# Expert-bias mix of a routed layer as two float32r matmuls on split parts, remainders in the rows that held zeros

## The reference

```python
logits = jnp.einsum('th,eh->te', flat, router_weight) + router_bias
scores = jax.nn.softmax(logits, axis=-1)
topk_w, topk_idx = jax.lax.top_k(scores, K_TOP)
w_sum = topk_w.sum(axis=-1, keepdims=True)
w_dense = jnp.zeros((T, E), dtype=scores.dtype).at[jnp.arange(T)[:, None], topk_idx].add(topk_w)
bias_mix = jnp.einsum('te,eh->th', w_dense, expert_bias)
out = flat * w_sum + bias_mix
```

## Time and profile before

| | before |
|---|---|
| median of 3 runs | 1754.7 us (1750.4 to 1756.32) |
| profiled execution | 1754.61 us, of it span 1752.8 us |
| PE | 1696.2 us busy, 97% of the span |
| PE weight loads | 1427.7 us, 81% |
| DVE | 871.8 us, 50% |
| ACT | 778.8 us, 44% |
| POOL | 298.5 us, 17% |
| mean granted TensorE clock | 0.992 |

### The profile page before, as it was taken

How to read it: one execution, slowest core, us unless ns; L and a number is a source line. 1 busy time by engine, 2 the same in 40 slices (tenths; PEclk the granted TensorE clock), 3 DMA queues, 4 the chain that set the end, 5 groups by cost and what they waited for, 6 DMA issues and landing times. The chain is left out here.

```text
span 1752.8 us, 25373 instructions
## 1 busy us (share of the span) xinstructions
PE 1696.2 (97%) x8546; PEld 1427.7 (81%) x8546; DVE 871.8 (50%) x2683; ACT 778.8 (44%) x2143; POOL 298.5 (17%) x669
## 2 busy tenths in 40 slices
PE   5888999999999999999999999999999999999999
PEld 4667897888888888888888888888888788888887
DVE  7776010555555555555556546556566553323212
ACT  4476434555455455445445536545545432121111
POOL 4611000221131122122112113112222000000000
PEclk9989999999999999999999999999999999999999
DMA  5200425111111101101101101100100231000000
GB/s 158 72 1 1 156 80 208 37 25 37 37 25 36 37 24 38 37 13 49 37 13 49 37 13 41 38 20 17 45 13 19 80 95 43 1 24 1 24 1 24
DMA packets 47001, 74.73 MB, mean 43 GB/s; under 512 B 4576, under 2 KB 23008, under 8 KB 44832
## 3 DMA queue, kind: packets, MB, share of 16 engines
q1 hardware_dynamic: 45984, 72.63, 13.0%
q10 hardware_dynamic: 896, 0.56, 0.1%
HBM read 52.20 MB, written 20.97 MB: 42 GB/s over the span
## 5 line engine op out<-in xcount | busy, mean ns | idle before, releaser
L961 POOL TENSOR_SCALAR prob<-prob,inv_sum 128x128 f32<-128x128 f32 x256 | 98.5, 385 | 829.3 <-DVE inv_sum L1104 829.3
L1199 PE MATMUL ps_q<-h_hi,kv_w_hi 128*128 128x512 f32 x512 | 205.7, 402 | 1.4 <-PEq L758 1.4
L989 ACT ACTIVATE prob<-prob,neg_max 128x128 f32<-128x128 f32 x256 | 100.7, 393 | 238.4 <-DVE neg_max L1099 238.4
L1199 PE MATMUL ps_q<-h_lo,kv_w_hi 128*128 128x512 f32 x512 | 200.1, 391 | 0.0
L1199 PE MATMUL ps_q<-h_hi,kv_w_lo 128*128 128x512 f32 x512 | 199.8, 390 | 0.0
L133 ACT ACTIVATE prob_t_hi<-ps_s 128x512 fp32r<-128x512 f32 x192 | 107.4, 598 | 73.9 <-PE ps_s L1248 73.9
L962 POOL TENSOR_SCALAR prob<-prob,inv_sum 128x256 f32<-128x256 f32 x256 | 136.9, 535 | 0.0
L1084 DVE TENSOR_TENSOR x<-ps_q,x 128x512 f32<-128x512 f32 x128 | 88.3, 690 | 97.6 <-PE ps_q L1277 97.6
L138 DVE TENSOR_TENSOR prob_t_lo<-ps_s,prob_t_hi 128x512 fp32r<-128x512 f32 x192 | 126.2, 685 | 15.1 <-ACT prob_t_hi L133 12.5
L1466 DVE SCALAR_TENSOR_TENSOR f_act<-f_ps_r,f_scale,f_act 128x512 f32<-128x512 f32 x44 | 33.0, 751 | 192.1 <-PE f_ps_r L1497 190.7
L991 ACT ACTIVATE prob<-prob,neg_max 128x256 f32<-128x256 f32 x256 | 127.2, 497 | 0.0
(11 more groups left out here) (184 smaller groups left out, 4244.8 us busy)
## 6 DMA issues: line engine op xcount, KB each, us to landing
k_scratch<-kv_stage SPq DMA_DIRECT2D x32, 256.0 KB, 2.4
v_scratch<-kv_stage SPq DMA_DIRECT2D x32, 256.0 KB, 2.0
w_raw<-in_wq_g SPq DMA_DIRECT2D x8, 1024.0 KB, 4.8
k_raw<-k_scratch SPq DMA_DIRECT2D x32, 256.0 KB, 3.5
v_raw<-v_scratch SPq DMA_DIRECT2D x32, 256.0 KB, 4.0
w_raw<-in_wo_g SPq DMA_DIRECT2D x8, 1024.0 KB, 6.2
x<-in_x SPq DMA_DIRECT2D x16, 256.0 KB, 2.9
out<-x SPq DMA_DIRECT2D x16, 256.0 KB, 2.1
```

The source lines that it names most:

```text
L961: pool.tensor_scalar(prob[:, b, h, 0:P], prob[:, b, h, 0:P], inv_sum[:, b, h, 0:1], 1.0, ALU.mult, ALU.mult)
L989: act.activation(prob[:, b, h, 0:P], prob[:, b, h, 0:P], ACT.Exp, scale=-1.0, bias=neg_max[:, b, h, 0:1], accum_out=row_sum[:, b, h, 0:1])
L1199: last = pe.matmul(ps_q[:, h % 2, :], wq[a][:, c, h * HEAD:(h + 1) * HEAD], h3[b][:, c, pair * PAIR:(pair + 1) * PAIR], start=(c == 0 and ...
```

## The change

The mix becomes two float32r matmuls. The expert biases are loaded twice, into rows 0 to 63 and 64 to 127. Once, at the stage's start, ACT rounds all 128 rows to float32r, and DVE replaces rows 64 to 127 by the remainder. `chosen` is written twice side by side (128 columns), so that after the transpose rows 64 to 127 of `chosen_t` repeat rows 0 to 63. ACT's copy rounds it to float32r; DVE subtracts the rounded part from the transposed weights in PSUM and writes the remainder of 64 rows into `chosen_lo`. Then one matmul over 128 rows gives rounded weights times (rounded + remainder of the biases), and a second over 64 rows adds the remainder of the weights times the rounded biases. The fourth product, of both remainders, is left out. A new semaphore `b_ctl_done` is set by DVE's subtraction; PE waits for it before the mix and, in place of `b_ctc_done`, before it writes the shared bank again. The two memsets of zeros are gone.

```diff
--- before.py
+++ after.py
@@ -463,7 +463,8 @@
     def load(self, eng, router_t, router_bias, expert_bias):
         eng.dma_start(self.router[:, :, :], router_t.rearrange("(c p) n -> p c n", p=P)).then_inc(self.loaded, 16)
         eng.dma_start(self.logit_bias[:, :], router_bias.partition_broadcast(P)).then_inc(self.loaded, 16)
-        eng.dma_start(self.expert_bias[0:EXPERTS, :], expert_bias).then_inc(self.loaded, 16)
+        for rows in (slice(0, EXPERTS), slice(EXPERTS, P)):
+            eng.dma_start(self.expert_bias[rows, :], expert_bias).then_inc(self.loaded, 16)
 
 
 class RoutedBias:
@@ -492,7 +493,9 @@
         self.one_zero = sb("r_one_zero", [P, 2], F32, st)
         self.combined = sb("r_combined", [P, 2, 2], F32, st)
         self.chosen = sb("r_chosen", [P, 2, P], F32, st)
-        self.chosen_t = sb("r_chosen_t", [P, 2, P], F32, st)
+        self.chosen_t = sb("r_chosen_t", [P, 2, P], F32R, st)
+        self.chosen_lo = sb("r_chosen_lo", [P, P], F32R, st)
+        self.bias_parts = sb("e_bias_parts", [P, HID], F32R, st)
         self.ps_t, self.ps_l, self.ps_m, self.ps_n = [bank[:, n, :] for n in range(4)]
         self.ps_c = self.ps_t
         self.zeroed = sem("b_zeroed")
@@ -512,6 +515,8 @@
         self.scaled_done = sem("b_scaled_done")
         self.ct_done = sem("b_ct_done")
         self.ctc_done = sem("b_ctc_done")
+        self.ctl_done = sem("b_ctl_done")
+        self.bias_hi_done, self.bias_lo_done = sem("b_bias_hi_done"), sem("b_bias_lo_done")
         self.mix_done = sem("b_mix_done")
         self.x_done = sem("b_x_done")
         self.h_next_done = sem("b_h_next_done")
@@ -523,15 +528,22 @@
         return self.ps_n.rearrange("p (c n) -> p c n", c=KC)
 
     def set_constants(self, pool):
-        for n, (part, value) in enumerate(((self.one_zero[:, 0:1], 1.0), (self.one_zero[:, 1:2], 0.0),
-                                           (self.weights.expert_bias[EXPERTS:P, :], 0.0), (self.chosen[:, :, EXPERTS:P], 0.0))):
+        for n, (part, value) in enumerate(((self.one_zero[:, 0:1], 1.0), (self.one_zero[:, 1:2], 0.0))):
             if n:
                 pool.wait_ge(self.zeroed, n)
             pool.memset(part, value).then_inc(self.zeroed, 1)
 
     def await_constants(self, eng):
-        eng.wait_ge(self.zeroed, 4)
-        eng.wait_ge(self.weights.loaded, 48)
+        eng.wait_ge(self.zeroed, 2)
+        eng.wait_ge(self.weights.loaded, 64)
+
+    def bias_hi_part(self, act):
+        hi_part(act, [self.bias_parts[:, :]], self.weights.expert_bias[:, :]).then_inc(self.bias_hi_done, 1)
+
+    def bias_lo_part(self, dve):
+        dve.wait_ge(self.bias_hi_done, 1)
+        low = self.bias_parts[EXPERTS:P, :]
+        lo_part(dve, [low, low], self.weights.expert_bias[EXPERTS:P, :]).then_inc(self.bias_lo_done, 1)
 
     def pool_body(self, pool, i, par, live):
         if live(6):
@@ -599,7 +611,8 @@
             dve.wait_ge(self.rest_done, t3 + 1)
             if not known(t3) or t3 >= 2:
                 dve.wait_ge(self.ct_done, t3 - 1)
-            dve.tensor_tensor(self.chosen[:, odd, 0:EXPERTS], self.e[:, odd, :], self.rest[:, odd, :], ALU.subtract).then_inc(self.chosen_done, 1)
+            twice = [part[:, odd, :].unsqueeze(1).to_broadcast([P, 2, EXPERTS]) for part in (self.e, self.rest)]
+            dve.tensor_tensor(self.chosen[:, odd, :].rearrange("p (n e) -> p n e", n=2), twice[0], twice[1], ALU.subtract).then_inc(self.chosen_done, 1)
             dve.wait_ge(self.inv_done, t3 + 1)
             dve.tensor_tensor(self.weight_sum[:, odd:odd + 1], self.top_sum[:, odd:odd + 1], self.inv_total[:, bass.ds(t3, 1)], ALU.mult).then_inc(self.sum_done, 1)
         if live(5):
@@ -607,6 +620,10 @@
             dve.wait_ge(self.scaled_done, t5 + 1)
             dve.scalar_tensor_tensor(tile_of(self.x, t5), self.ps_m, self.inv_total[:, bass.ds(t5, 1)], tile_of(self.x, t5),
                                      ALU.mult, ALU.add).then_inc(self.x_done, 1)
+        if live(4):
+            t4 = i - 4
+            dve.wait_ge(self.ctc_done, t4 + 1)
+            lo_part(dve, [self.chosen_t[0:EXPERTS, par, :], self.chosen_lo[0:EXPERTS, :]], self.ps_c[0:EXPERTS, 0:P]).then_inc(self.ctl_done, 1)
         if live(3):
             dve.wait_ge(self.sum_done, t3 + 1)
             if not known(t3) or t3 >= 2:
@@ -633,7 +650,7 @@
             if live(2):
                 pe.wait_ge(self.ht_done, i - 2 + 1)
             else:
-                pe.wait_ge(self.ctc_done, i - 4)
+                pe.wait_ge(self.ctl_done, i - 4)
             pe.transpose(self.ps_c[:, 0:P], self.chosen[:, par, :], self.ident[:, :]).then_inc(self.ct_done, 1)
         if live(9):
             t = i - 9
@@ -645,10 +662,13 @@
             last.then_inc(self.tn_done, 1)
         if live(5):
             t = i - 5
-            pe.wait_ge(self.ctc_done, t + 1)
+            pe.wait_ge(self.ctl_done, t + 1)
             if not known(t) or t >= 1:
                 pe.wait_ge(self.x_done, t)
-            pe.matmul(self.ps_m, self.chosen_t[:, odd, :], self.weights.expert_bias[:, :], start=True, stop=True).then_inc(self.mix_done, 1)
+            else:
+                pe.wait_ge(self.bias_lo_done, 1)
+            pe.matmul(self.ps_m, self.chosen_t[:, odd, :], self.bias_parts[:, :], start=True, stop=False)
+            pe.matmul(self.ps_m, self.chosen_lo[0:EXPERTS, :], self.bias_parts[0:EXPERTS, :], start=False, stop=True).then_inc(self.mix_done, 1)
         if live(2):
             t = i - 2
             pe.wait_ge(self.ht_done, t + 1)
@@ -662,7 +682,7 @@
             t = i - 1
             pe.wait_ge(self.h_done, t + 1)
             if not known(i) or i - 4 >= 0:
-                pe.wait_ge(self.ctc_done, i - 4 + 1)
+                pe.wait_ge(self.ctl_done, i - 4 + 1)
             elif t >= 1:
                 pe.wait_ge(self.ht_done, t)
             for c in range(KC):
@@ -809,6 +829,8 @@
 
                             stream.hi(act, wq, query_weights[n], 0)
 
+                act.wait_ge(weights.loaded, 64)
+                routed.bias_hi_part(act)
                 interleaved(act, routed.act_body, task)
 
             @block.vector
@@ -823,6 +845,7 @@
                     if n in query_weights:
                         stream.lo(dve, wq, query_weights[n], 0)
 
+                routed.bias_lo_part(dve)
                 interleaved(dve, routed.dve_body, task)
 
             @block.tensor
```

## The result

| | before | changed |
|---|---|---|
| median (4 runs each on one chip) | 1754.63 us (1750.4 to 1756.32) | 1775.65 us (1775.3 to 1776.24) |
| ratio, 95% interval | | 1.0124 [1.0106, 1.0142] |
| profiled execution, its span | 1754.61, 1752.8 us | 1775.85, 1774.1 us |
| mean granted TensorE clock | 0.992 | 0.976 |

The change makes the kernel 21 us slower; the forecast was 1757.8 us, the range ended at 1766. The page of the changed kernel says where to look: the clock row has 5 and 6 tenths in the third and fourth slices, 89 to 177 us.

What follows compares the result with a forecast made beforehand. In the routed stage PE was taken to bound early iterations, DVE those from 9, PE again between projections. Terms of +0.4, +0.2, -1.7, +0.8, +1.7, -1.5 sum to -0.1; with +3.3 for the clock, 1754.6 becomes 1757.8 us, range 1749.5 to 1766.

Steps and rivals of the forecast that it cites:

- The clock: Routed stage: the return from half clock, at about 104 us before, comes three iterations later, +3.3 us.
- rival A: Clock stays at half or falls back through most of the routed stage: slower, 1769.8 us; chance 0.24.
- The two mixes at half clock: Iterations 5 and 6: two float32r matmuls take 0.86 us for 1.72, -1.7 us in all.
- the four at full clock: Mixes between projections: two float32r slots take 0.48 us for 0.86, four times -0.38, -1.5 us.
- Rival C: The float32r matmul isn't cheaper in this form, so the mix gains are missing: 1761 us; chance 0.02.
- The new wait: PE's transposes of h wait for DVE's remainder behind x: iterations 7 and 8 take 3.67 us for 3.29, +0.8.
- DVE's own work: Iterations 9 to 16: DVE pays 0.20 and 0.07 more, 3.95 us for 3.68, x no longer waits; +1.7 us.
- The start: Second load of expert biases at program start, +0.4 us; ACT's rounding before its first h at stage start, +0.2.
- Rival B: PE's chain sets the pace everywhere, each mix in iterations 7 to 16 gives 0.38 back: 1748.2 us; chance 0.06.

Runs made afterwards that it cites:

- e9: Changed kernel with two more 64-row float32r matmuls per mix into a spare bank, up to iteration 15, x waiting for them: 1785.19 us, ratio 1.0176.
- e2: Changed kernel without DVE's remainder and its waits; the second matmul takes the rounded weights again: 1776.97 us, ratio 1.0132.
- e6: e5 with two more 128-row float32r matmuls into an unused bank behind each mix up to iteration 15: 1755.48 us, ratio 1.0020.
- e5: Changed kernel with the weights' remainder taken on all 128 rows and the second matmul over 128 rows: 1759.54 us, ratio 1.0037.
- e7: Changed kernel with unused matmuls filling PE's pauses as in e3, and 3 in the loop's iterations too: 1754.46 us, ratio 1.0004.
- e1: Kernel before, float32 mix kept, plus DVE's 64x128 subtraction (result unused) and PE's waits for it: 1761.06 us, ratio 1.0039.
- e8: Kernel before with the same filling of unused matmuls as e7, loop's iterations included: 1747.41 us, ratio 0.9969.
- e3: Changed kernel with unused matmuls in PE's pauses: 18 behind the first stage, 3 in each of iterations 1 to 9: 1763.89 us, ratio 1.0054.
- e11: e5 with the remainder on DVE ahead of the x update, chosen_lo double, chosen single, no filling: 1752.62 us, ratio 1.0008.
- e4: Kernel before with the same unused matmuls in PE's pauses as e3: 1747.34 us, ratio 0.9964.
- e10: e5 with the remainder on DVE ahead of the x update, chosen_lo double, chosen single, plus e7's filling: 1748.88 us, ratio 0.9967.

## Why the prediction was wrong

**The clock** is the step that failed. I took three further iterations at half clock; it was all of them. What happened is rival A, to which I gave 0.24. I had written that the share of an iteration in which PE is busy would fall and that this made the return uncertain, yet by the records the share hardly moved: (5.39 - 0.78) / 5.39 = 0.855 before, (5.14 - 0.78) / 5.14 = 0.848 after. With the one the clock came back within two such iterations; with the other it did not in four, nor in the seven behind them, at 36.58 / 41.76 = 0.876, and e9 stayed at half with 0.87. So the share busy as the records count it did not say whether the clock would return; that it would say so was my assumption. Less the two loads of 0.28 us under no matmul the share is (5.14 - 0.78 - 0.57) / 5.14 = 0.74 after and 0.775 in e9, for 0.855 before (an estimate from these rows), so in that sense it did fall, for a reason that I had not seen. The runs show that the mix with a matmul over 64 rows kept the clock low (0.50 up to about 167 us in e2 and 175 in e9, against 100 in e6); whether by its rows or by its loads stays open.

**The two mixes at half clock, and the four at full clock**, were mis-sized by one thing, the slot. I took that of the same type and width in the projections, but their matmuls have 128 rows on both sides. Measured 1.41 for 0.86 and 0.82 for 0.48. The term of -1.5 in the tail was 0; that of -1.7 was 2 x -0.2 by the periods (5.18 and 5.14 for 5.39). With full rows (e5) the tail's term came as forecast. Rival C, "not cheaper in this form", which I gave 0.02, was nearly true. The slot is also why A's own figure was low, 1769.8 for 1775.7: 5.14 for 4.53 in iterations 5 to 8 and 5.97 for 5.41 in 9 to 15 make 2.4 + 3.9 = 6.3 us.

**The new wait** was right in place and size: at full clock 3.70 us per iteration (e7) for my 3.67, against 3.28. But it holds for iterations 5 to 8, not for 7 and 8 alone, once the clock is up. e1 shows 0.47 where I worked out 0.38.

**DVE's own work**: the remainder 0.19 for my 0.20. The sum of iterations 9 to 15 was not right, 28.7 us in e7 for my 27.65: I had x no longer wait for the mix, and it still waits 0.33, because the mix is not shorter.

**The start**: +1.2 for +0.6. The rounding itself costs 0.5 before h, where the sum had 0.2 for it and the memsets together, and the rest comes with the second load; that share rests on a comparison of profiles.

**Rival B** is refuted: with the clock up in both, the iterations 5 to 15 of the changed form (e7, 3.70 to 4.18 us) are each longer than the same one of the old form (e8, 3.22 to 3.90).

Of the 21.0 us: 14.0 by the clock, 7.1 by the change's waits, work and start once the filling is in (nearer 5 at full clock throughout), where the forecast's terms without the clock came to about zero.

**Open**: whether it is the 64 rows or the two uncovered loads that keep the clock low. A kernel with full rows and pauses of 0.28 us in the same two places would tell; it wasn't tried. e9 also has x wait for its matmuls while e6 has not, and e5 is not only fuller in rows than the changed kernel but has shorter iterations. Open too is why the iterations of e3 without filling let the clock fall while those of before and e5 hold it: e3 had PE busy for 9.47 of 12.42 us (76%) in the three iterations before the fall, e5 for 13.86 of 19.82 (70%) in iterations 11 to 15, at 1.00 throughout.

Short falls of some 3 us came right behind longer pauses of PE: in e1, e2, e6 and e11 behind one of 0.95 to 1.1 us and one of 1.3 to 1.4, 2.4 us apart (between 157 and 187 us), in before at 1387 us behind 1.20 and 2.05 us, so that it was not work alone that failed to hold the clock there, as I had taken it for rival A. Yet before has pauses of 1.10 and 1.26 us at 161.5 and 163.9 too, and kept 1.00. A remainder at the changed kernel's 64 rows in the early place wasn't tried.

## What to carry to other kernels

Before shortening TensorE's work in a stage where TensorE pauses, look at the granted clock there, and price the stage at half clock for its whole length: that price (iterations 9 to 15: 41.76 us for 26.26), not the saved slot, was the size of this change. Where the clock is low in such a stage, matmuls nobody uses in the pauses are worth trying by themselves: on the kernel before they gave 0.36% (e4, 1747.3 us, the fastest median here with e8 and faster than both kernels). A matmul over 64 of 128 rows among ones over 128 was no half of one here, 0.72 us at half clock for 0.43 over 128 rows: pad it to the full height where the rows are there, and put a remainder that frees a shared bank ahead of an instruction that waits, not behind it (the two together, e10 against e7: 1748.9 us for 1754.5).

## What was new of the hardware

What these runs measured, each with its run:

- A matmul over 64 rows between two over 128 took longer than one over 128 rows in its place: slots 0.69 and 0.72 us for the two of the mix in the changed kernel, 0.56 and 0.43 in e5, at half clock; 0.40 and 0.42 for 0.32 and 0.23 at full. In the changed kernel its weight load and the next one started with their own slots (101.89 and 102.61 us), in e5 0.42 us ahead of them (100.13 and 100.56 for the slots 100.55 and 100.98). In e9 the load of a 64-row matmul behind another of 64 started at 102.88 us, under the matmul of 102.71, and those where the height changes at 102.71 and 104.28, with their slots: in these records it is the change of height that costs.
- With three 64-row matmuls in each mix (e9) the granted clock stayed 0.50 for some 95 us (80 to 175 us) with PE busy for 87% of iteration 6; with the same number of matmuls over full rows (e6) it was back at 100 us.
- More work on PE made kernels faster: e6 (1755.48 us) by 4 us over e5 (1759.54), e4 (1747.34) by 7 over before (1754.63).
- The granted clock also fell in a stage that had it: e3 at 123.1 us, with PE busy for 76% of the three iterations before. PE's busy time alone did not tell when: e5 kept 1.00 with 70% (124.09 to 143.91 us).
